# Tower of token features, attention and experts: matmuls regrouped into 64x64 and 32x64 array tiles, accumulator banks exchanged between row halves, periodic features computed ahead of the loop

## Chip, cores, metric

One core of one Trainium2 chip runs the whole program. The metric is the device time of the execution in microseconds (us). The time before is the median of three runs.

## What is computed

Sixteen sequences of 512 tokens, 64 channels. All arithmetic is float32.

```python
# periodic features: 4 id streams, 3 harmonics, sin and cos -> 24 numbers a token
ang = 2*pi*t/period * harmonic + phase;  x = [w*sin(ang), w*cos(ang)]
h   = layernorm(relu(x@W1+b1)@W2+b2)*gamma + beta + 0.1*(x@Wres+bres)
# attention, 8 heads; the context is laid out (head*64+d, position), not the usual way
n = layernorm(h);  k = n@Wk.T;  v = n@Wv.T
attn = softmax(q @ k * scale);  ctx = attn @ v;  h = h + ctx_as_(512,512) through Wo
# top-2 of 6 experts, three 64x64 layers each, gated by a router (64 -> 32 -> 6)
f = layernorm(h);  logits = softmax(relu(f@rw1+rb1)@rw2+rb2);  top 2, softmax of the two
h = h + sum_over_top2(weight * expert(f))
```

## The kernel before

The sequences are handled in eight pairs. `body(i)` in each engine's program walks through 64 slots of pair i. An even slot issues `scores` (L437): four matmuls in 64x64 tiles, each moving 512 columns, into one of three ring buffers `s_bank` (two PSUM banks each). VectorE takes the row maximum of each half (L812) and ScalarE the exponential with its sum (L698), which frees the buffer. Eight slots make one step `a`: 8 x 128 rows of probabilities `p`. For each step `pv` (L464) multiplies the transposed reciprocal sums times output weights (`woz`, made by GpSimd, L300) with `p` into `m_bank`, in two parts of 32 matmuls, at slots 12 and 15 modulo 8. These work in tiles of 128 rows and 32 columns, each matmul moving 128 columns. VectorE then turns `m_bank` into `m` (L824). This is attention re-associated: output weights first, values last. The value product `FIN` (L551) multiplies all of `m` with the values `v` in 16 matmuls of 512 columns into a bank of its own, `f_bank`, and VectorE adds it to `h` as `hatt` (L993).

The other work of the loop is laid into the slots by hand-written tables: `P` for the preparation of pair i+1 (`H1` and `TOK` of the feature network, the layer norms, `T` the transposes at L522, `V` the values), `F` for the rest of pair i-1 (`FIN`, layer norm, `T` transposes L565, `R` router L570, `L` logits L578, `GATE` 22 small VectorE operations, `E1`, `E2`, `Y` expert layers), `Z` the same within the last pair's body, and `L` for the last pair's own tail, after the loop. Before the change `XT` transposes, `R`, `L` and `FIN` use `f_bank`; everything else uses the ring in the order that `ring_order` gives. A matmul that needs a ring buffer waits (`free`) until the entry three places earlier has been read. `m` has one copy only, so the first turn of a pair waits for `FIN` of the pair before (`turn`).

The periodic features (`reduced`, L335, nine VectorE steps, then `sines` on ScalarE and `weigh`) are made in three groups of columns: pair 0 and pair 1 ahead of the loop, 256 columns each, and pairs 2 to 7 (1536 columns) inside `body(0)`, one step every six slots (`FOUR_AT`). A float32 matmul is two instructions in the trace ("passes"), so a count there is twice the count in the code. `warm` issues matmuls on a spare tile whose result nobody reads.

## Time and profile before

| | |
|---|---|
| median of three runs | 755.57 us (755.11 to 757.14) |
| profiled execution | 755.78 us |
| its span | 754.0 us |
| TensorE (PE) busy | 698.5 us, 93% |
| VectorE (DVE) busy | 552.8 us, 73% |
| ScalarE (ACT) busy | 477.7 us, 63% |
| GpSimd (POOL) busy | 289.2 us, 38% |
| start of the first scores | 31.4 us |
| body(0), first scores to first scores of body(1) | 86.6 us |
| body(1) to body(6), each | 86.35 us |
| last body, then the tail | 82.5 us, 35.4 us |

The span is what the profiler saw from the first to the last instruction, 1.8 us less than the execution's own time. Busy shares of TensorE are of modelled ends: two starts in the timeline give a better duration than the length printed for one row.

### The profile page before, as it was taken

The numbers are of one execution on the slowest core, as the hardware profiler recorded it, in microseconds if no ns is written. First come the engines' busy times: TensorE is split into PE (matmuls) and PEld (weight loads), VectorE is DVE, ScalarE is ACT, GpSimd is POOL, SyncE is SP. The second block draws the span as 40 slices with busy tenths as digits, with TensorE's granted clock in tenths as the row PEclk, the third lists the DMA queues.
The fourth block names the chain that finished last, engine by engine and source line by source line (L and its number), as shares of the span: only waits on it lengthen the run. The fifth ranks groups of instructions, "written<-read, shape, count | busy, mean of one in ns | idle before, by whom it ended". The sixth has DMA issues, their size and how long they took to land.

```text
span 754.0 us, 31976 instructions
## 1 busy us (share of the span) xinstructions
PE 698.5 (93%) x14256; PEld 388.7 (52%) x14256; DVE 552.8 (73%) x1069; ACT 477.7 (63%) x1206; POOL 289.2 (38%) x362
## 2 busy tenths in 40 slices
PE   6689879999999999999999999999999999999985
PEld 6344436554555546454554555555455555454662
DVE  6488655878768786877778677777878687677835
ACT  2377675686567766676666766577656875676613
POOL 1143021531566118531466317550376216422702
PEclk9699989999999999999999999999999999999999
DMA  4000000000000000000000000000000000000000
GB/s 167 1 2 3 2 2 3 3 2 3 4 17 3 2 3 3 17 3 2 4 17 3 2 3 4 17 3 3 3 17 3 3 2 4 17 3 3 3 17 16
DMA packets 9449, 7.27 MB, mean 10 GB/s; under 512 B 8672, under 2 KB 8800, under 8 KB 9184
## 3 DMA queue, kind: packets, MB, share of 16 engines
q1 hardware_dynamic: 9312, 5.23, 2.4%
q8 instruction: 112, 1.84, 1.0%
q14 instruction: 25, 0.20, 0.1%
HBM read 3.13 MB, written 2.10 MB: 7 GB/s over the span
## 4 chain that ended last, share of the span: by engine, by line
PE 66%; DVE 17%; ACT 6%; POOL 5%; issue 5%; ACTq 0%; DVEq 0%; POOLq 0%
PE m_bank L464 25%; PE s_bank L437 21%; DVE nmax L812 7%; ACT p L698 4%; PE f_bank L551 3%; PE s_bank L589 3%; PE s_bank L449 3%; PE s_bank L600 2%; PE s_bank L622 2%; DVE st L829 1%; POOL st L1100 1%; DVE e2t L1008 1%; DVE y L1023 1%; PE s_bank L522 1%; PE m_bank L659 1%
## 5 line engine op out<-in xcount | busy, mean ns | idle before, releaser
L698 ACT ACTIVATE p<-s_bank,nmax 128x512 f32<-128x512 f32 x512 | 347.2, 688 | 208.0 <-DVE nmax L812 207.1
L812 DVE TENSOR_REDUCE nmax<-s_bank 128x1 f32<-128x512 f32 x512 | 325.9, 681 | 101.1 <-PE s_bank L437 100.0
L437 PE MATMUL s_bank<-kf,g 64*64 64x512 f32 x2048 | 266.3, 608 | 11.8 <-ACT p L698 8.9
L464 PEld LDWEIGHTS m_bank<-p,woz 128*32 128x32 f32 x8192 | 219.3, 111 | 101.7 <-issue 101.2
L464 PE MATMUL m_bank<-p,woz 128*32 128x128 f32 x8192 | 253.1, 276 | 3.2 <-POOL woz L300 3.1
L300 POOL TENSOR_TENSOR woz<-cst,rz 128x256 f32<-128x256 f32 x126 | 75.9, 624 | 281.2 <-DVE rz L818 281.2
L437 PEld LDWEIGHTS s_bank<-kf,g 64*64 64x64 f32 x2048 | 65.6, 134 | 126.1 <-issue 53.8
L698 ACT ACTIVATION_READ_ACCUMULATOR p<-s_bank,nmax 128x1 f32 x512 | 103.8, 203 | 0.0
L824 DVE STREAM_TRANSPOSE m<-m_bank 128x512 f32<-128x512 f32 x64 | 45.7, 714 | 33.5 <-PE m_bank L464 33.3
L1100 POOL TENSOR_TENSOR st<-st,power 128x8 f32<-128x8 f32 x24 | 40.0, 1668 | 68.8 <-DVE st L839 68.8
L309 POOL TENSOR_TENSOR y<-y,gt 128x768 f32<-128x768 f32 x28 | 41.4, 1477 | 27.9 <-DVE y L1023 26.0
L449 PE MATMUL s_bank<-kf,qk 64*64 64x512 f32 x256 | 35.0, 617 | 8.0 <-ACT p L698 4.9
L1023 DVE TENSOR_TENSOR y<-s_bank,cst 128x768 f32<-128x768 f32 x28 | 26.7, 952 | 15.1 <-PE s_bank L622 11.0
L317 POOL TENSOR_TENSOR ys<-y 128x384 f32<-128x384 f32 x30 | 30.2, 1006 | 17.3 <-DVE y L1034 15.1
L622 PE MATMUL s_bank<-cst,e2t 64*64 64x64 f32 x1536 | 28.7, 220 | 6.6 <-DVE e2t L1008 4.6
L622 PEld LDWEIGHTS s_bank<-cst,e2t 64*64 64x64 f32 x1536 | 25.5, 134 | 17.6 <-issue 13.1
L704 ACT COPY g<-s_bank 128x1024 f32<-128x1024 f32 x32 | 32.4, 1013 | 2.2 <-PE s_bank L449 2.2
L1008 DVE TENSOR_SCALAR e2t<-s_bank,cst 128x512 f32<-128x512 f32 x42 | 29.5, 745 | 4.1 <-PE s_bank L600 4.1
L747 ACT ACTIVATE e1t<-s_bank,cst 128x1024 f32<-128x1024 f32 x24 | 26.7, 1114 | 6.1 <-PE s_bank L589 6.0
L551 PE MATMUL f_bank<-m,v 128*32 128x512 f32 x224 | 27.7, 595 | 0.0
L589 PE MATMUL s_bank<-xt,cst 64*64 64x512 f32 x192 | 26.1, 613 | 1.3 <-ACT p L698 1.3
L709 ACT ACTIVATE sq<-xc 128x512 f32<-128x512 f32 x24 | 15.0, 625 | 18.9 <-DVE xc L851 17.7
(118 smaller groups left out, 499.6 us busy)
## 6 DMA issues: line engine op xcount, KB each, us to landing
tower_out<-o SPq DMA_DIRECT2D x16, 128.0 KB, 2.6
cst<-consts SPq DMA_DIRECT2D x1, 1198.0 KB, 8.9
e2t<-ids SPq DMA_DIRECT2D x1, 896.0 KB, 5.9
cst<-consts SPq DMA_DIRECT2D x1, 544.0 KB, 4.1
cst<-consts SPq DMA_DIRECT2D x1, 288.0 KB, 6.3
e2t<-ids SPq DMA_DIRECT2D x1, 128.0 KB, 2.5
cst<-consts SPq DMA_DIRECT2D x1, 3.5 KB, 2.2
```

What stands on the lines that cost most here:

```text
L300: ops.tensor_tensor(woz[:, kept, four, :].rearrange("q (m h) c -> q m h c", h=2), k("wo").rearrange("q (m c) -> q m c", m=4)[:, 2 * n:2 * ...
L309: ops.tensor_tensor(yt, yt, gt[:, 8, two, :].unsqueeze(3).to_broadcast([128, 2, NE, C]), ALU.mult).then_inc(y_pool, 1)
L437: last = pe.matmul(double[half(q), 512 * r:512 * r + 512], g[half(r), a // 2 % 2, a % 2, first:first + 64], kf[half(r), par, a // 4, :], s ...
L449: last = pe.matmul(double[half(q), 512 * r:512 * r + 512], qk[half(r), 2 * (quad % 2) + q, :], kf[half(r), par, quad // 2, :], start=True, ...
L464: last = pe.matmul(m_bank[quarter(r), 128 * n:128 * n + 128], woz[:, kept, 2 * mm + hh, 32 * oh:32 * oh + 32], keys[:, r, :, :], start=(mm ...
L551: last = pe.matmul(f_bank[quarter(2 * b2 + q), :], v[:, par, b2, jj, quarter(q)], m[:, b2, :, jj, :], start=(jj == 0), stop=(jj == 3))
L589: last = pe.matmul(double[half(q), 512 * r:512 * r + 512], k("e1")[half(r), first:first + 64], xt[half(r), :], start=True, stop=True)
L622: last = pe.matmul(double[half(q), 512 * c + C * x:512 * c + C * x + C], e2t[half(c), x, first:first + 64], k("e3")[half(c), C * x:C * x + ...
L698: nc.scalar.activation(p[:, 8 * kept + c % 8, :], bank("S", i, c - r)[:, 512 * r:512 * r + 512], ACT.Exp, bias=nmax[:, c % 16:c % 16 + 1], ...
L812: nc.vector.tensor_reduce(nmax[:, c % 16:c % 16 + 1], bank("S", i, c - r)[:, 512 * r:512 * r + 512], AX.X, ALU.max, negate=True).then_inc( ...
L824: nc.vector.transpose(m[:, b2, n:n + 4, :, :].rearrange("q n j o -> q (n j o)"), m_bank[:, :]).then_inc(mtd, 1)
L1100: nc.gpsimd.tensor_tensor(st[n][:, 4, :], st[n][:, 3, :], power[:, :], ALU.pow).then_inc(ln_step[n], 1)
```

## The change

In words:
- `pv` works in 64x64 tiles: the 128 rows of `p` are split into two row halves, and each matmul moves 256 columns, 16 matmuls a part. In part 0 row half 0 writes bank `hh=0` of `m_bank` and half 1 bank `hh=1`; in part 1 they swap banks and add, after a wait on `pv_half`. `m_bank` is two banks now, and `f_bank` is gone.
- The second feature layer (`TOK`) does the same exchange (`tok_half`), in 64x64 tiles. The transposes `T` and `XT` become matmuls with an identity in 64x64 tiles (`turn_halves`). The router and the logits are in 64x64 tiles too.
- `FIN` becomes `value_products`: 128 matmuls of 128 columns in 32x64 tiles, in two parts with the exchange wait `fin_half`. It writes two ring buffers, `FIN 0` and `FIN 1`; `XT`, `R` and `L` take a ring buffer each.
- Features: seven steps instead of nine; two groups, pair 0 (256 columns) and pairs 1 to 7 (1792 columns), both ahead of the loop. Four steps of the second group stand before the first layer norm, one in each layer norm, one behind; then VectorE also copies half of `kf` and `g` (`first_copies`). The weighting of the second group is GpSimd's.
- `xn` is stored once instead of twice. The first warm-up has 18 matmuls (24 before), the second 13 (8 before), the second starting one small operation earlier. The slot tables have new numbers.

```diff
-WARM0, WARM, WARM_T = 24, 8, 20
-FOUR_AT, FOUR_SINE, FOUR_WEIGH = (2, 8, 14, 20, 26, 32, 38, 44, 50), 56, 56
+WARM0, WARM, WARM_T = 18, 13, 20
-F = {'FIN': (8, 12, 13, 14),
- 'LN': 14,
+F = {'FIN': 15,
+ 'LN': 15,
...
     def ffn(i, slot, f):
+        if f is not L and slot == f["FIN"]:
+            order.extend([("FIN", i, 0), ("FIN", i, 1)])
+        for name, first in (("XT", "T"), ("R", "R"), ("L", "L")):
+            if slot == f[first]:
+                order.append((name, i))
...
-            if step in (4, 5, 6):
-                ins = stt(out=A, in0=T, scalar=-(c1, c2, c3)[step - 4], in1=A, op0=ALU.mult, op1=ALU.add)
-            if step == 7:
-                ins = ts(A, A, shift, pi, ALU.add, ALU.min)
-            if step == 8:
-                ins = ts(A, A, -pi, None, ALU.max)
+            if step in (4, 5):
+                ins = stt(out=A, in0=T, scalar=-(c1, c2)[step - 4], in1=A, op0=ALU.mult, op1=ALU.add)
+            if step == 6:
+                ins = ts(A, A, least, most, ALU.max, ALU.min)
...
-            def pv(i, a, hh):
+            def pv(i, a, part):
...
-                if hh == 0:
+                if part == 0:
                     wait(pe, mtd, HH * i + a)
                     pe.wait_ge(wozd, 2 * (HH * i + a) + 2)
-                for oh in range(2):
-                    n = 2 * hh + oh
-                    for mm in range(4):
-                        keys = p[:, 8 * kept + 2 * mm + hh, :].rearrange("q (j r o) -> q r j o", j=4, r=4)
-                        for r in range(4):
-                            last = pe.matmul(m_bank[quarter(r), 128 * n:128 * n + 128],
-                                             woz[:, kept, 2 * mm + hh, 32 * oh:32 * oh + 32], keys[:, r, :, :],
-                                             start=(mm == 0), stop=(mm == 3), skip_group_check=True)
-                last.then_inc(pvd, 1)
+                else:
+                    pe.wait_ge(pv_half, HH * i + a + 1)
+                for mm in range(4):
+                    for r in range(2):
+                        hh = (r + part) % 2
+                        keys = p[half(r), 8 * kept + 2 * mm + hh, :].rearrange("q (n h o) -> q h n o", n=8, h=2)
+                        for q in range(2):
+                            last = pe.matmul(m_bank[half(q), 512 * hh:512 * hh + 256], woz[half(r), kept, 2 * mm + hh, :],
+                                             keys[:, q, :, :], start=(part == 0 and mm == 0), stop=(part == 1 and mm == 3),
+                                             skip_group_check=True)
+                last.then_inc(pvd if part else pv_half, 1)
+            def turn_halves(double, part, count):
+                for t in range(count):
+                    for r in range(2):
+                        for c in range(2):
+                            last = pe.matmul(double[half(c), 512 * r + C * t:512 * r + C * t + C], part(t, half(r), c),
+                                             k("ident")[half(r), half(r)], start=True, stop=True,
+                                             skip_group_check=True)
...
+            def value_products(i, par, first, end, part, start, stop):
+                for n in range(8):
+                    for g4 in range(4):
+                        q, s2 = g4 // 2, g4 % 2
+                        odd = (q + part) % 2
+                        for b2 in range(2):
+                            last = pe.matmul(
+                                bank("FIN", i, s2)[half(b2), 512 * odd + 16 * first:512 * odd + 16 * end],
+                                v[quarter(g4), par, b2, n, :],
+                                m[quarter(g4), b2, first + odd:end:2, n, :],
+                                start=(start and n == 0), stop=(stop and n == 7), skip_group_check=True)
...
             def fin_part(n):
...
-                heads, cols = ((slice(0, 8), slice(0, 256)), (slice(8, 12), slice(256, 384)),
-                               (slice(12, 16), slice(384, 512)))[n]
+                first, end = ((0, 4), (4, 6), (6, 8))[n]
...
+                value_products(i, par, first, end, 0, True, False).then_inc(fin_half, 1)
+                pe.wait_ge(fin_half, i + n + 1)
+                value_products(i, par, first, end, 1, False, True).then_inc(fin_parts, 1)
...
-                    for q in range(4):
-                        last = pe.matmul(f_bank[quarter(q), :], k("rw1")[:, quarter(q)], xt[:, :], start=True, stop=True)
+                    free("R", i)
+                    for c in range(2):
+                        for r in range(2):
+                            last = pe.matmul(bank("R", i)[half(c), 512 * r:512 * r + 256], k("rw1")[half(r), half(r)],
+                                             xt[half(r), 256 * c:256 * c + 256], start=True, stop=True)
```

The order of TensorE's matmuls in a body of the loop, slots 7 to 16 of body(1) (`m_bank<-p,woz` is `pv`, `s_bank<-kf,g` scores, `<-kf,qk` a query product, `<-feat,cst` and `<-cst,h1t` the feature network, `<-m,v` the value product; counts are matmuls of the code). Before:

```order
L464 MATMUL m_bank<-p,woz 32x128 x32
L502 MATMUL s_bank<-cst,feat 64x128 x16
L437 MATMUL s_bank<-kf,g 64x512 x4
L511 MATMUL s_bank<-cst,h1t 32x64 x32
L551 MATMUL f_bank<-m,v 32x512 x4
L437 MATMUL s_bank<-kf,g 64x512 x4
L449 MATMUL s_bank<-kf,qk 64x512 x4
L437 MATMUL s_bank<-kf,g 64x512 x4
L464 MATMUL m_bank<-p,woz 32x128 x32
L551 MATMUL f_bank<-m,v 32x512 x8
L437 MATMUL s_bank<-kf,g 64x512 x4
L551 MATMUL f_bank<-m,v 32x512 x4
```

And in the changed kernel, the same slots:

```order
L483 MATMUL m_bank<-p,woz 64x256 x16
L452 MATMUL s_bank<-kf,g 64x512 x4
L531 MATMUL s_bank<-cst,feat 64x128 x16
L546 MATMUL s_bank<-cst,h1t 64x64 x32
L452 MATMUL s_bank<-kf,g 64x512 x4
L464 MATMUL s_bank<-kf,qk 64x512 x4
L452 MATMUL s_bank<-kf,g 64x512 x4
L483 MATMUL m_bank<-p,woz 64x256 x16
L452 MATMUL s_bank<-kf,g 64x512 x4
L483 MATMUL m_bank<-p,woz 64x256 x16
L568 MATMUL s_bank<-m,v 64x128 x128
L452 MATMUL s_bank<-kf,g 64x512 x12
```

The value product moved from three places among the scores (4, 8 and 4 matmuls) into one piece of 128 behind the second part of the products, and its target is the ring.

The order of VectorE's work from the second feature group to the first layer norm, ahead of the loop. Before, with group 1 being pair 1 alone:

```order
L341 TENSOR_SCALAR feat<-e2t,per_turn 128x256
L345 TENSOR_SCALAR feat<-feat,cst 128x256
L347 TENSOR_SCALAR e1t<-feat,cst 128x256
L349 TENSOR_SCALAR e1t<-e1t 128x256
L351 SCALAR_TENSOR_TENSOR feat<-e1t,feat 128x256 x3
L353 TENSOR_SCALAR feat<-feat,cst 128x256
L355 TENSOR_SCALAR feat<-feat 128x256
L361 TENSOR_SCALAR feat<-e1t,cst 128x256
L829 TENSOR_REDUCE st<-s_bank 128x8
L831 TENSOR_SCALAR st<-st 128x8
L851 TENSOR_TENSOR xc<-s_bank,st 128x512
```

And in the changed kernel, the second group, with pieces of the first and second layer norm of pair 0 around it:

```order
L346 TENSOR_SCALAR feat<-e2t,per_turn 128x1792
L350 TENSOR_SCALAR feat<-feat,cst 128x1792
L352 TENSOR_SCALAR e1t<-feat,cst 128x1792
L354 TENSOR_SCALAR e1t<-e1t 128x1792
...
L888 TENSOR_SCALAR st<-st 128x8
L356 SCALAR_TENSOR_TENSOR feat<-e1t,feat 128x1792
L918 TENSOR_TENSOR tok<-xc,cst 128x8x64
L921 TENSOR_TENSOR xc<-tok,st 128x512
...
L356 SCALAR_TENSOR_TENSOR feat<-e1t,feat 128x1792
L901 TENSOR_TENSOR xn<-xc,st 128x512
L358 TENSOR_SCALAR feat<-feat,cst 128x1792
L938 COPY kf<-s_bank 128x512
```

The weighting of pair 1 went to GpSimd, and two 1792-column multiply-adds (L356) stand inside the layer norms, each ahead of an operation that the first transposes wait for.

TensorE's last products and value products, in the tail. Before:

```order
L464 MATMUL m_bank<-p,woz 32x128 x32
L538 MATMUL f_bank<-m,v 32x256 x16
L464 MATMUL m_bank<-p,woz 32x128 x64
L538 MATMUL f_bank<-m,v 32x128 x32
L659 MATMUL m_bank<-spare 128x128 x20
```

And in the changed kernel:

```order
L483 MATMUL m_bank<-p,woz 64x256 x16
L568 MATMUL s_bank<-m,v 64x64 x128
L483 MATMUL m_bank<-p,woz 64x256 x32
L568 MATMUL s_bank<-m,v 64x32 x256
L708 MATMUL m_bank<-spare 128x128 x20
```

The three pieces of the last value product stay where they were, with 128 matmuls each in place of 16.

## Rows read from the trace of the kernel before

**Rows 1.** Windows, bodies 0 and 3: PE, PEld, DVE, ACT, POOL busy, clock, DMA, GB/s.

```profile
31.40:118.00 86.60, 73.97 (x1308) 39.51 (x1312) 61.06 (x97) 59.58 (x147) 20.57 (x23) 0.91 0.01 2
...
290.70:377.05 86.35, 83.69 (x1772) 45.50 (x1764) 66.30 (x130) 58.10 (x149) 38.15 (x48) 1.00 0.02 6
```

**Rows 2.** Timeline of TensorE in body(3): start, length, line, tiles, passes.

```profile
304.23 1.04 PE L449 MATMUL s_bank<-kf,qk 64*64 64x512 f32 x8
305.09 1.04 PE L437 MATMUL s_bank<-kf,g 64*64 64x512 f32 x8
306.06 1.96 PE L464 MATMUL m_bank<-p,woz 128*32 128x128 f32 x64
307.83 1.90 PE L551 MATMUL f_bank<-m,v 128*32 128x512 f32 x16
309.66 1.09 PE L437 MATMUL s_bank<-kf,g 64*64 64x512 f32 x8
310.68 1.06 PE L551 MATMUL f_bank<-m,v 128*32 128x512 f32 x8
311.56 1.93 PE L464 MATMUL m_bank<-p,woz 128*32 128x128 f32 x64
313.42 2.81 PE L437 MATMUL s_bank<-kf,g 64*64 64x512 f32 x24
```

**Rows 3.** The same timeline: logits, expert outputs, both with the next, first feature layer.

```profile
334.38 0.44 PE L578 MATMUL f_bank<-cst,rh 128*32 128x12 f32 x32
334.75 1.09 PE L437 MATMUL s_bank<-kf,g 64*64 64x512 f32 x8
...
375.60 1.63 PE L622 MATMUL s_bank<-cst,e2t 64*64 64x64 f32 x96
377.05 1.90 PE L437 MATMUL s_bank<-kf,g 64*64 64x512 f32 x16
...
382.10 1.09 PE L491 MATMUL s_bank<-feat,cst 64*64 64x256 f32 x16
```

**Rows 4.** TensorE's waits within body(0): in total, times, longest.

```profile
PE s_bank L437 <- ACT p L698: 8.9, 5, 4.8
```

**Rows 5.** Timeline of TensorE in body(0); in brackets idle time ahead and releaser.

```profile
78.38 3.50 PE L464 MATMUL m_bank<-p,woz 128*32 128x128 f32 x64
...
109.93 1.98 PE L437 MATMUL s_bank<-kf,g 64*64 64x512 f32 x8 [4.76 <-ACT p L698]
111.84 3.64 PE L464 MATMUL m_bank<-p,woz 128*32 128x128 f32 x64
```

**Rows 6.** Windows of 7.2 us in body(4), columns as in rows 1.

```profile
398.64:405.83 7.19, 6.87 (x140) 3.65 (x132) 6.87 (x15) 4.53 (x12) 5.65 (x6) 1.00 0.01 2
405.83:413.03 7.20, 6.63 (x108) 3.15 (x108) 6.80 (x12) 4.71 (x14) 2.67 (x4) 1.00 0.00 0
```

**Rows 7.** Ahead of and in body(0): feature steps on VectorE, a copy on ScalarE.

```profile
8.00 0.35 DVE L341 TENSOR_SCALAR feat<-e2t,per_turn 128x256 f32<-128x256 int32 x1
...
12.10 0.41 DVE L361 TENSOR_SCALAR feat<-e1t,cst 128x256 f32<-128x256 f32 x1 [0.48 <-ACT e1t L786]
...
30.36 1.01 ACT L704 COPY g<-s_bank 128x1024 f32<-128x1024 f32 x1 [2.18 <-PE s_bank L449]
...
35.76 1.01 DVE L341 TENSOR_SCALAR feat<-e2t,per_turn 128x1536 f32<-128x1536 int32 x1
...
64.28 1.75 DVE L351 SCALAR_TENSOR_TENSOR feat<-e1t,feat 128x1536 f32<-128x1536 f32 x1
```

**Rows 8.** Timeline of the tail: last products, value products, VectorE's sum.

```profile
716.69 1.91 PE L538 MATMUL f_bank<-m,v 128*32 128x256 f32 x32
...
718.68 3.75 PE L464 MATMUL m_bank<-p,woz 128*32 128x128 f32 x128
...
722.17 2.15 PE L538 MATMUL f_bank<-m,v 128*32 128x128 f32 x64
...
724.39 0.69 DVE L993 TENSOR_TENSOR h<-h,f_bank 128x512 f32<-128x512 f32 x1 [1.20 <-PE f_bank L538]
```

More of the change, by code:

```diff
@@ L540, in fin_part @@
[L540 to L554 removed]
+                    free("FIN", i, 0)
```

365 lines of the change are left out of this document (192 added, 173 removed).

## The prediction

> **What bounds the kernel now.** I read the windows first, one a body of the loop [rows 1]: in body(3) TensorE is busy for 83.69 of 86.35 us at full clock, so it idles 2.66 us, while VectorE is busy for 66.30 and ScalarE for 58.10. body(0) is another case: 73.97 of 86.60 us busy at a mean clock of 0.91, though it has no expert work in it. So the six equal bodies are bound by TensorE, and body(0) partly by something else.
>
> Next the timeline of TensorE, to see what its time is made of. I take start to next start. A product of 512 columns with 64x64 tiles on both sides takes 305.09 - 304.23 = 0.86 us; 0.97 if the next work is in 128x32 tiles; 1.02 with such work on both sides (309.66 to 310.68). A part of the probability product takes 1.77 if the next work has the same tiles (306.06 to 307.83) and 1.86 if it is scores again (311.56 to 313.42) [rows 2]. So leaving one tile shape costs about 0.11 us and entering the next 0.05: 0.16 us a switch, and nearly every part of the products has one on each side. There are 40 switches in each of bodies 1 to 6, 33 in body(0) and 37 in the last (counted in the order of matmuls).
>
> **The change, part by part.**
>
> *Products in 64x64.* Columns moved over tiles are the same: 32 x 128 / 4 before, 16 x 256 / 4 after. Is a 256-column matmul in 64x64 tiles at full rate? The first feature layer is one: its 16 passes, after a switch, have the length of 1.09 us [rows 3] that the 8 passes of 512 columns at 309.66 have after one [rows 2]. So a part costs 1.71 us (two times 0.855), and the products themselves give nothing but their switches. The wait between the two parts costs nothing, since scores stand between them, except in the tail.
>
> *Switches.* In a body, `TOK`, `T`, `XT`, `R`, `L` are in 64x64 too; only the value product (32x64) is left, two switches. 38 x 0.16 = 6.1 us less a body.
>
> *Router.* Four matmuls of 256 columns in place of four of 512, in four tiles: -0.43 us.
>
> *Transposes, logits.* Expert outputs run 96 passes of 64 columns in 377.05 - 375.60 = 1.45 us, 15.1 ns a pass [rows 3]. `T` is 64 such passes, 0.97 us, `XT` 32, 0.48; before they took 1.02 and 0.59 with a switch in each. Nothing to gain or lose, nor for the logits (as many passes as before).
>
> *Value product.* 256 passes of 128 columns in eight tiles. Before: 16 passes in 309.66 - 307.83 = 1.83 us with one switch, so 3.4 for all. No row shows eight tiles or 32 rows. 
>
> Sum for TensorE's work in a body: 83.69 - 6.1 - 0.4 + 0.3 = 77.5 us.
>
> *What is late next.* VectorE keeps its 66.3 us [rows 1], 86% of 77.5, and in the stretch behind the old value product it is already busy for 13.67 of 14.39 us, with TensorE idling 0.89 [rows 6]. Now the value product holds two of three ring buffers for 3.6 us at slot 15; VectorE waits for it with the next turn (one copy of `m`), and turn, sum and mean (each about as long as the sum of 0.69 us in [rows 8]) pile up behind it, ahead of the maxima that free the scores' buffers. So idle time grows. By the rows: the stretch of rows 6 holds 13.50 us of TensorE's work, seven switches (1.1) go from it, and 12.4 stand against VectorE's 13.67, so 1.3 us of waiting; behind the value product one score block (0.86) covers most of turn and first half sum (1.1 to 1.4), 0.4 is left; the waits elsewhere stay at 2.66 - 0.89 = 1.8. That is 3.5 us a body. Low end: the 2.66 of now. High end: if half of the body's work ran like rows 6, 1.3 us of waiting to 12.4 of work, that half had 4.1; with the 0.4, and the 1.8 of elsewhere, it is 6.3. Then a body takes 81.0 us, 5.35 less; six of them **-32.1**.
>
> *The last body* has 35 switches less (5.6), the router's 0.4, and the same new waits (+1): **-5.0**.
>
> *body(0).* Waits of scores for exponentials are 8.9 us in five [rows 4]. 4.8 is the sine in the loop with its two table loads (109.93), the rest but 0.3 stands behind multiply-adds of 1.75 us on VectorE [rows 7]. All go with the features. After the two longest TensorE's clock is down: product parts of 3.50 and 3.64 us in place of 1.96, scores of 1.98 in place of 1.09 [rows 5]; that is 4.1 us. Switches: 33 x 0.16 = 5.3. So 86.6 - 8.6 - 4.1 - 5.3 = 68.6 us. TensorE would then have about 3 us of idle time and 3 of half clock left in it, and VectorE 61.06 - 11.3 = 50 us of work (three steps of 1.75, six of about 1.0 [rows 7]). With 1.2 us of new waits: **-16.8**. If the dense phase costs as much as elsewhere, -14; if the first scores are at full clock, -19.
>
> *Ahead of the loop.* Group 1 took VectorE from 8.00 to 12.51, right up to the first layer norm; four wide steps at 1.01 x 1792 / 1536 = 1.18 us are 4.7 us in the same place [rows 7]: +0.2. Each of the two multiply-adds of 1792 columns costs 1.75 x 1792 / 1536 = 2.0 us, partly under GpSimd's power function: I take +0.5 together, and +0.3 for `T` at half clock. Then one `xn` operation instead of two, -0.8 (one sum's length, 0.7, and a semaphore); `kf` and `g` copied by two engines in place of one, half of 1.01 us [rows 7] each, -1.0. The sine of group 2 stands under the query product. Sum **-0.8**. The weights' product on GpSimd is due five slots later, and hidden.
>
> *The tail.* The three pieces of the value product are 128 matmuls each now, of 64 and 32 columns. At such widths passes cost 11.6 to 15.1 ns whatever they move, 3.0 to 3.9 us a piece. The first took 1.91 [rows 8]; its excess of 1.5 lies partly beside exponentials and `woz`, for which the products behind it wait; I take 1.0. The other two ran from 722.17 to 724.3; now 6.5, +4.3. The exchange in the last products +0.2, router, transposes and six switches -1.0: **+4.5**.
>
> **Sum.** -32.1 - 5.0 - 16.8 - 0.8 + 4.5 = -50.2. The profiled execution's own time was 755.78 us, 0.2 above the median shown; 755.6 - 50.2 = **705.4 us**.
>
> **Rivals.**
>
> *A: VectorE and the ring become the bound.* For it: rows 6, the value product's two ring buffers, and five more ring entries a body. Against: over a whole body VectorE has 11 us to spare even at 77.5, and its waits aren't all bunched. With 7 us of idle time a body instead of 3.5 (from 6.3 on I call it A), seven bodies give back 24: 730 us. The Trainium skill says the same of tiling ("TensorEngine Tiling (Array Packing)", PSUM Bottleneck: it "speeds up TensorE but not PSUM evacuation"). Here the windows say the margin is thin but there.
>
> *B: only four of the eight tiles run side by side.* +3.4 us in each of seven value products = 24, and 3 in the tail: 732 us. For it: no row shows 32-row tiles. Against: everything else obeys columns over tiles.
>
> *C (other side): the row groups of 32 don't overlap at all.* Then two tiles work at once, 53 ns a pass, 13.7 us a value product, +10.2 x 7 = 71, and 3 in the tail: 780 us, slower. It decides from 10.5 us a value product on, 41 ns a pass. Against: 64-row halves do overlap, or the scores would take twice as long.
>
> *D: TensorE's waits stay at 2.66 us a body, and body(0) gains 3 more* (first scores at full clock). 0.84 x 7 + 3 = 9 less: 696 us. For it: the 11 us of slack just named.
>
> **How the numbers follow.** Forecast (700 to 718) 0.56, A 0.16, B 0.10, C 0.03, D 0.12; A and B together 0.03, of which 0.02 within 0.3% and 0.01 slower. The range goes from D's far side to B, 688 to 733, leaving out C, half of what is left of A above it, and the 0.03: about 0.15. Within 0.3% is what a measurement of this kernel can't tell from no change. Faster 0.94, same 0.02, slower 0.04.
>
> **What would show it.** Product parts 1.71 us from start to start, scores 0.86 wherever they stand. The bodies' period 79 to 83 us. A value product of 3.4 to 3.9 us in two pieces; 6.8 is B, 13.7 is C. Idle waits of scores on VectorE or on exponentials, mostly in slots 16 to 28: above 7 us a body is A. body(0) under 72 us without a row of half clock after its first 6 us. From the end of the last products to VectorE's sum 6 to 8 us against 2.2. The prediction is wrong if a product part keeps 1.85 us in spite of one tile shape: then weight loads of 64 columns aren't hidden at 256 columns, and some 20 us come back.

## The result and the profile after

The changed kernel takes 773.58 us (median of 4 runs, 772.83 to 776.52), the kernel before 755.34 beside it: ratio 1.0244, 95% interval 1.0213 to 1.0276. It is slower; the forecast was 705.4 us. The profiled execution took 772.83 us with a span of 771.0, 17.0 more than before. The windows of body(0), body(4) and the last body, against [rows 1] (columns as there):

```profile
32.58:101.61 69.03, 64.42 (x928) 32.48 (x932) 50.69 (x88) 54.16 (x142) 18.38 (x22) 0.98 0.01 2
366.36:455.06 88.70, 80.40 (x1566) 42.61 (x1561) 66.25 (x131) 58.18 (x147) 36.84 (x47) 1.00 0.02 6
632.59:720.96 88.37, 78.64 (x1629) 42.57 (x1621) 61.94 (x123) 52.82 (x139) 37.00 (x52) 1.00 0.04 9
```

body(0) shrank by 17.6 us. A full body has 3.3 us less of TensorE's work than before (80.40 against 83.69), and is 2.3 us longer, since it idles 8.3 us where it idled 2.7. The first piece of the last value product stands ahead of the last products, so its +1.0 of the prediction is counted in the fourth row. Cut into the prediction's terms (from stretch to stretch of both traces):

| stretch | before | after | moved | predicted |
|---|---|---|---|---|
| ahead of the first scores | 31.42 | 32.58 | +1.2 | -0.8 |
| body(0) | 86.6 | 69.0 | -17.6 | -16.8 |
| bodies 1 to 6 | 518.1 | 531.0 | +12.9 | -32.1 |
| last body, up to the last products | 82.6 | 88.4 | +5.8 | -4.0 |
| from there to the end | 35.3 | 50.0 | +14.7 | +3.5 |

TensorE in body(4), around the value product (timeline; in brackets the idle time ahead and its releaser):

```profile
384.89 3.06 PE L568 MATMUL s_bank<-m,v 32*64 32x128 f32 x167
388.79 1.58 PE L568 MATMUL s_bank<-m,v 32*64 32x128 f32 x89 [0.84 <-issue]
390.31 1.09 PE L452 MATMUL s_bank<-kf,g 64*64 64x512 f32 x8
391.62 1.95 PE L452 MATMUL s_bank<-kf,g 64*64 64x512 f32 x16 [0.23 <-DVE hatt L1055]
...
396.01 1.09 PE L452 MATMUL s_bank<-kf,g 64*64 64x512 f32 x8 [0.71 <-ACT p L747]
...
402.47 1.09 PE L452 MATMUL s_bank<-kf,g 64*64 64x512 f32 x8 [1.99 <-ACT p L747]
403.38 1.04 PE L464 MATMUL s_bank<-kf,qk 64*64 64x512 f32 x8
404.74 1.09 PE L452 MATMUL s_bank<-kf,g 64*64 64x512 f32 x8 [0.33 <-ACT p L747]
```

The value product takes 390.31 - 384.89 = 5.4 us, 0.84 of it a gap for which the trace names no releaser ("issue"). Behind it come four waits, 3.3 us; eight more in the rest of the body, of 0.20 to 0.77, make 3.95. The gap has a place of its own: in bodies 1 to 5 it stands behind 252, 224, 195, 167 and 138 of the 256 passes, 28 or 29 earlier from one body to the next. VectorE over the same place:

```profile
390.49 0.72 DVE L873 STREAM_TRANSPOSE m<-m_bank 128x512 f32<-128x512 f32 x1 [5.23 <-PE s_bank L568]
...
391.21 0.70 DVE L1055 TENSOR_TENSOR hatt<-h,s_bank 128x256 f32<-128x256 f32 x2
391.94 0.69 DVE L878 TENSOR_REDUCE st<-hatt 128x8 f32<-128x512 f32 x1
...
392.74 2.48 DVE L861 TENSOR_REDUCE nmax<-s_bank 128x1 f32<-128x512 f32 x4
...
397.84 1.57 DVE L960 SCALAR_TENSOR_TENSOR h<-tok,xc 128x512 f32<-128x512 f32 x1
```

It idles 5.23 us during the value product and has then turn, sums and mean to do before the next maxima. The tail, TensorE's timeline, for [rows 8]:

```profile
715.52 2.48 PE L568 MATMUL s_bank<-m,v 32*64 32x64 f32 x177
719.92 1.11 PE L568 MATMUL s_bank<-m,v 32*64 32x64 f32 x79 [1.93 <-issue]
720.96 4.00 PE L483 MATMUL m_bank<-p,woz 64*64 64x256 f32 x64
724.89 1.35 PE L568 MATMUL s_bank<-m,v 32*64 32x32 f32 x112
727.62 1.95 PE L568 MATMUL s_bank<-m,v 32*64 32x32 f32 x128 [1.38 <-issue]
731.10 0.47 PE L568 MATMUL s_bank<-m,v 32*64 32x32 f32 x16 [1.52 <-issue]
731.78 1.81 PE L568 MATMUL s_bank<-m,v 32*64 32x32 f32 x111 [0.21 <-PE s_bank L568]
735.71 2.42 PE L568 MATMUL s_bank<-m,v 32*64 32x32 f32 x128 [2.12 <-issue]
739.18 0.47 PE L568 MATMUL s_bank<-m,v 32*64 32x32 f32 x17 [1.06 <-issue]
741.29 7.01 PE L708 MATMUL m_bank<-spare 128*128 128x128 f32 x40 [1.64 <-DVE st L878]
```

Two pieces that move 32 columns a pass last 14.9 us, from 724.89 until VectorE's sum begins at 739.76, and six of these are gaps. From the start behind one gap to the start behind the next it is 2.7 to 4.6 us. So two questions: what makes the gaps, and what makes the waits in the bodies?

### The profile page after: what moved, and what is told of

The parts are those of the page before. It is cut to its first block, busy times and chain, and to the rows that moved or that the text cites. A ratio compares the mean times of both kernels' runs of the same rounds, so it can differ in the third digit from the quotient of the medians.

```text
span 771.0 us, 29600 instructions
## 1 busy us (share of the span) xinstructions
PE 675.2 (88%) x13070; PEld 371.0 (48%) x13070; DVE 548.0 (71%) x1064; ACT 472.9 (61%) x1186; POOL 281.3 (36%) x354
## 3 DMA queue, kind: packets, MB, share of 16 engines
q1 hardware_dynamic: 9312, 5.23, 2.3%
q8 instruction: 103, 1.69, 0.9%
## 4 chain that ended last, share of the span: by engine, by line
PE 56%; DVE 23%; issue 7%; ACT 6%; POOL 6%; DMA 1%; SPq 0%; ACTq 0%; DVEq 0%; POOLq 0%
PE m_bank L483 20%; PE s_bank L452 18%; DVE nmax L861 9%; PE s_bank L568 6%; ACT p L747 4%; DVE e2t L1070 3%; PE s_bank L649 2%; PE s_bank L638 2%; PE s_bank L464 2%; DVE y L1085 2%; POOL y L316 2%; DVE st L878 2%; POOL st L1158 1%; DVE h L960 1%; ACT e1t L795 1%
## 5 line engine op out<-in xcount | busy, mean ns | idle before, releaser
L483 PE MATMUL m_bank<-p,woz 64*64 64x256 f32 x4096 | 244.5, 376 | 2.4 <-POOL woz L307 2.3
L483 PEld LDWEIGHTS m_bank<-p,woz 64*64 64x64 f32 x4096 | 158.0, 133 | 119.1 <-issue 67.1
L452 PEld LDWEIGHTS s_bank<-kf,g 64*64 64x64 f32 x2048 | 68.9, 133 | 143.8 <-ACT p L747 50.7
L1158 POOL TENSOR_TENSOR st<-st,power 128x8 f32<-128x8 f32 x24 | 42.9, 1788 | 90.1 <-DVE st L888 90.1
L758 ACT ACTIVATE sq<-xc 128x512 f32<-128x512 f32 x24 | 15.1, 629 | 86.0 <-POOL xc L1153 47.8
L568 PE MATMUL s_bank<-m,v 32*64 32x128 f32 (+2 forms) x2560 | 43.6, 268 | 14.6 <-issue 13.7
L568 PEld LDWEIGHTS s_bank<-m,v 32*64 32x64 f32 x2560 | 37.2, 138 | 22.6 <-issue 19.8
L1085 DVE TENSOR_TENSOR y<-s_bank,cst 128x768 f32<-128x768 f32 x28 | 26.6, 950 | 13.6 <-PE s_bank L671 7.9
L708 PE MATMUL m_bank<-spare 128*128 128x128 f32 x102 | 18.4, 363 | 12.3 <-DVE st L878 11.4
```

Of the source, the lines that this page charges most:

```text
L452: last = pe.matmul(double[half(q), 512 * r:512 * r + 512], g[half(r), a // 2 % 2, a % 2, first:first + 64], kf[half(r), par, a // 4, :], s ...
L483: last = pe.matmul(m_bank[half(q), 512 * hh:512 * hh + 256], woz[half(r), kept, 2 * mm + hh, :], keys[:, q, :, :], start=(part == 0 and mm ...
L568: last = pe.matmul(bank("FIN", i, s2)[half(b2), 512 * odd + 16 * first:512 * odd + 16 * end], v[quarter(g4), par, b2, n, :], m[quarter(g4) ...
L1158: nc.gpsimd.tensor_tensor(st[n][:, 4, :], st[n][:, 3, :], power[:, :], ALU.pow).then_inc(ln_step[n], 1)
```

## The experiments

There are eighteen kernels. A time without a ratio is that of a single execution. A "period" is the time from one body's value product to the next; it is 86.34 us before and 88.5 after.

### Half the matmuls in the value product, and a quarter

`e1_fin64`: 64 matmuls of 256 columns, a bank for each group of rows, no exchange, four half-width sums on VectorE.

```diff
-    bank("FIN", i, s2)[half(b2), 512 * odd + 16 * first:512 * odd + 16 * end],
+    bank("FIN", i, s2)[half(b2), 512 * q + 32 * first:512 * q + 32 * end],
     v[quarter(g4), par, b2, n, :],
-    m[quarter(g4), b2, first + odd:end:2, n, :],
+    m[quarter(g4), b2, first:end, n, :],
```

> The changed kernel with the value product as 64 matmuls of 256 columns in place of 128 of 128: each row group of 32 keeps a bank of its own and works all eight heads, the two partial sums are added by VectorE (four half-width sums in place of two), no exchange wait. Same columns, half the instructions. Theory I (small matmuls outrun the supply of TensorE's instructions): a value product falls from 5.4 us to about 3.6, the gap of 0.8 us in it goes, the two last pieces of the tail from 14.8 to some 7 us; 7 x 1.8 + 8 = about 20 us less, 753 us. Theory II (the tiles of 32 rows don't run eight at a time, whatever the instructions): a value product stays at 4.4 to 5.4 us, 6 to 10 us less from the tail alone. VectorE's two more sums cost up to 0.7 us a body in both.

Measured: 759.66 us (7 runs), ratio 1.0076 (1.0047 to 1.0105), still a little slower than the kernel before. TensorE in two bodies:

```profile
222.51 1.09 PE L452 MATMUL s_bank<-kf,g 64*64 64x512 f32 x8 [1.99 <-ACT p L740]
...
382.42 3.71 PE L565 MATMUL s_bank<-m,v 32*64 32x256 f32 x128
386.06 1.09 PE L452 MATMUL s_bank<-kf,g 64*64 64x512 f32 x8
388.12 1.95 PE L452 MATMUL s_bank<-kf,g 64*64 64x512 f32 x16 [0.96 <-DVE hatt L1049]
...
398.95 1.86 PE L452 MATMUL s_bank<-kf,g 64*64 64x512 f32 x8 [1.99 <-ACT p L740]
```

The value product is 3.64 us and its gap is gone, but the sums are now waited for 0.96 us, and the waits behind stay. The period is 87.65 in bodies 1 and 2, and 88.8 in the next three: there the scores behind the same 1.99 us run at half clock (1.86 in place of 1.09, granted clock 0.55). Most of the 15 us gained is the tail's: from its first piece to the end 44.1 us instead of 55.5. Theory I had the value product and the gap right; of its 20 us, the waits for the sums and the half clock took back a part.

`e2_fin_quarter`: the changed kernel with `for n in (0, 7)` in place of `range(8)`. It leaves out three quarters of the value product.

> The changed kernel with a quarter of the value product's matmuls (two of eight groups of keys; the rest is left out, so the attention's sum is incomplete). Theory III (the value product in one piece holds VectorE and ScalarE up, and the waits of scores behind it come from that): a body loses the 4.1 us of the piece and 2 to 3 us of waits behind it; with 13 us in the tail 712 us. Theory IV (the waits come from the ring's new entries XT, R and L and stay): 4.1 x 7 + 13 = 42 less, 731 us.

Measured: 731.16 us, period 85.1, with the waits behind it still 0.30, 1.03, 1.99 and 0.33. With a quarter of the value product left, a body is 3.4 us shorter, and the waits stay. That is Theory IV's number, but not yet its cause: whether the entries of the ring make the waits is asked below.

### The gaps by themselves

Spare matmuls take the place of, or follow, the 20 in front of `XT` in the tail, where nothing else runs.

```diff
+for cols in (32, 128):
+    for n in range(512):
+        r, q = n // 2 % 2, n % 2
+        pe.matmul(m_bank[half(q), 512 * r:512 * r + cols], spare[half(r), 0:64],
+                  spare[half(r), 0:cols], start=True, stop=True, skip_group_check=True)
```

That is the first of them; a matmul is two passes in the trace.

`e8_supply` (64 rows, 32 and then 128 columns):

> The changed kernel with its 20 spare matmuls in the tail replaced by 512 spare ones of 32 columns and then 512 of 128 columns, in 64x64 tiles, all four tiles in rotation, nothing to wait for and no other work on the chip beside them. Theory of supply: TensorE gets its instructions 256 at a time, and passes that are shorter than the supply leave gaps labelled issue after every 128 passes (two instructions each), at both sizes; the tail of the changed kernel had 112 to 128 passes every 2.7 to 4.6 us, so each group of 512 takes 11 to 18 us, the 32 columns not much less than the 128. Rival, that the passes themselves are the limit: 512 at the 17.2 ns of the value product are 8.8 us for 128 columns and less for 32, with no gaps. The whole is some 20 to 35 us longer than the changed kernel.

`e12_supply32` (64 rows, then 32 rows, of two row groups):

> The changed kernel with spare matmuls behind the 20 of the tail: first 256 of 128 columns in tiles of 64 rows, then 256 of 128 columns in tiles of 32 rows (512 passes each; a matmul is two passes). Supply theory: about 3.7 us for each 128 passes whatever the tile, 15 us a group, 30 together, and the passes of 32 rows show larger gaps, since they run at 17 ns when they run. Rival, that loading 64 rows of weights sets the 27 ns a pass seen in the run before: the group of 32 rows takes 512 times 17.2 ns, 8.8 us, with no gaps. The whole: 773 plus 28 to 32, or plus 22 to 24.

`e16_supply_first32` (32 rows first):

> The changed kernel with 256 spare matmuls of 128 columns in tiles of 32 rows behind the 20 of the tail, and then 256 in tiles of 64 rows: the order of the earlier run turned round. Supply theory: 27.8 us for 1024 passes as before in total; the first 100 to 128 passes of 32 rows, whose instructions are already there, run at 17 ns each, and then come gaps or the steady 27 to 28 ns. Rival, that 27 to 28 ns is what such a pass costs TensorE: 27.8 ns from the first pass on, and no gap.

Measured: 825.63, 801.15 and 802.95 us. In `e12_supply32`, 64 rows and then 32:

```profile
748.05 14.25 PE L606 MATMUL m_bank<-spare 64*64 64x128 f32 x512
762.23 14.43 PE L610 MATMUL m_bank<-spare 32*64 32x128 f32 x512
```

`e17_supply_four` uses four groups of rows with a bank each, so eight tiles, as the value product does:

> The changed kernel with 512 spare matmuls (1024 passes) of 128 columns behind the 20 of the tail, in tiles of 32 rows and now over all four groups of rows with a bank each, as the value product has them; the earlier runs used two groups of rows and went at 27 to 28 ns a pass from the first on, with a gap of 0.23 us after each 128 only late. Supply theory: as in the value product, the first 128 or so go at 17 ns, then a gap ends each 128, 3.5 to 3.75 us from one start to the next, 28 to 30 us for the 1024: 801 to 803 in all. Rival, that two groups of rows made the 27 ns and the supply never binds: 17.2 ns throughout, 17.6 us, no gaps, 790 to 792.

```profile
749.44 3.09 PE L606 MATMUL s_bank<-spare 32*64 32x128 f32 x199
753.50 2.08 PE L606 MATMUL s_bank<-spare 32*64 32x128 f32 x128 [0.97 <-issue]
756.97 2.08 PE L606 MATMUL s_bank<-spare 32*64 32x128 f32 x128 [1.39 <-issue]
760.72 2.08 PE L606 MATMUL s_bank<-spare 32*64 32x128 f32 x128 [1.66 <-issue]
```

Measured: 800.9 us. This is the supply: 199 passes, 13.8 ns from one start to the next, and from then on a gap, 128 passes in 2.08 us, a gap, and the next 128, 3.47 or 3.75 us from start to start, six times over. 128 passes are 256 instructions (weights and matmul). The page of the changed kernel's profile counts what was fetched for all engines:

```profile
q8 instruction: 103, 1.69, 0.9%
```

1.69 MB in 103 packets is 16.4 KB each. The trace of `e17_supply_four` has these packets one by one. All the DMA traffic from 753.4 to 776.9 us, in 40 slices and by queue:

```profile
GB/s 0 28 0 0 0 0 0 28 0 0 0 0 0 0 28 0 0 0 0 0 28 0 0 0 0 0 28 0 0 0 0 0 28 0 0 0 0 0 28 0
q8 instruction: 7, 0.11, 2.0%
```

There are seven gaps, the first just ahead of this stretch, and seven packets in it, one in each group of passes. A packet starts 1.05 to 1.15 us after its group has begun, takes 0.9 to 1.4 us, and the next group begins 1.2 to 1.6 us after it has ended: together the 3.5 to 3.75 us. The DMA engines are 2% busy meanwhile, so what is waited for looks like a round trip and not like a full DMA queue. In the value product of body(4) a packet ends at 387.44 and the gap at 388.79. And the gap follows the count of instructions, not the time: in all seven value products it stands behind the same number of passes in `e10_max_half`, `e11_exp_half` and `e19_both_half`, whose bodies are 0.8 to 4 us shorter.

The Trainium skill ("Runtime: NRT & Kernel Launch", Instruction fetch mechanics) says that instructions are fetched in blocks of 16 KiB, 256 instructions, and that this is hidden since engines dispatch more slowly than blocks arrive. The block agrees with the gaps. That it is hidden does not hold here, where TensorE takes 256 instructions in 2.08 us and gets them every 3.47 or 3.75.

### The entries of the rotation

`e4_before_ring`: the kernel before, with `XT`, `R` and `L` in the rotation.

```diff
+        for name, first in (("XT", "T"), ("R", "R"), ("L", "L")):
+            if slot == f[first]:
+                order.append((name, i))
```

> The kernel before with another part alone: the transposes XT, the router R and the logits L take a ring buffer each, the value product keeps its own bank. Theory IV (ring entries): at least 1 us of new waits a body, 762 us or more. Theory III (the value product's piece): under 0.5 us a body, within 755 to 759 us.

Measured: 799.11 us, ratio 1.0575 (1.0543 to 1.0608), period about 92.5. Its largest new wait:

```profile
338.88 1.99 PE L446 MATMUL s_bank<-kf,g 64*64 64x512 f32 x8 [2.57 <-ACT rh L769]
```

In the old order of the work three more entries cost 6 us a body. New waits are 4.3 of them; behind the one shown the clock is granted at 0.50, and the scores take 1.99 us in place of 1.09. Is it so in the changed kernel? `e5_xt` and `e7_all` start from `e1_fin64` and take `XT`, or `XT`, `R` and `L`, out again, into the bank of the products between two fillings.

```diff
-            if slot == f[first]:
+            if slot == f[first] and not (f is F and name in IN_M_BANK):
...
+                    pe.wait_ge(mtd, turned[0])
```

> The version with the value product in 64 matmuls (759.7 us), with the turns of the mixture (XT) of six bodies taken out of the rotation: they go to the bank of the products between two of its fillings (PE waits for the transpose of the products before, the next products wait for the copy of XT). One entry of the rotation less in each of six bodies. Ring-entry theory: the six together cost about 6 us a body in the old kernel, 1.5 to 2 us an entry, so 9 to 12 us less: 748 to 751, with the waits of the scores for exponentials (21.8 us over the run) down to 14 or less. Rival, that the waits come from the value product and the layer norm alone and go wherever there is room: 757 to 762. Rival, that the bank of the products is too tight a place: the products wait for the copy of XT about 1 us a body, 760 to 766.

> The same with all three of XT, R and L of six bodies outside the rotation, in the bank of the products between its fillings; XT two slots later, R one earlier, L two later, and the gates one slot later. Three entries less a body: by the ring-entry theory what the old kernel lost by them (43 us over the run, 6 us in each of seven bodies) comes back in six bodies, less what the products now wait: 725 to 738. Rival (the waits come from elsewhere): 757 to 762. Rival (new waits of the products for R's and L's readers, 1 us each): 745 to 755.

Measured: 762.05 (ratio 1.009, 1.0071 to 1.0109) and 760.94 us (1.007, 1.0052 to 1.0088). The waits of scores for exponentials fell from 21.8 to 9.8 and 9.2 us over the run, and more was waited for the place instead (15.7 us in six bodies). In `e7_all`:

```profile
402.18 1.13 PE L507 MATMUL m_bank<-cst,x 64*64 64x64 f32 x32 [2.61 <-DVE m L880]
```

`e9_none` adds an empty entry behind `R`, for which PE waits and which it doesn't use:

> The version with the value product in 64 matmuls, with one empty entry more in the rotation behind R in each of six bodies: no matmul uses it, PE only waits until it would be free. Ring-entry theory: one more entry costs what one costs elsewhere, 1.5 to 2 us a body, 769 to 772. Rival (entries cost nothing, work and its readers do): 758 to 762.

Measured: 758.81 us, period 88.3. This entry costs at most 0.7 us a body (88.3 against 87.65), and nothing in the whole. I had thought after `e4_before_ring` that the number of entries was the cause; in the changed kernel neither this entry more nor the one and three fewer of `e5_xt` and `e7_all` bear that out. That the 6 us in the old one came from where the readers stood in its order (`R`'s copy three slots behind `R`) is argued from the wait above and wasn't tried alone.

### Whose work is late

`e10_max_half`, `e11_exp_half` and `e19_both_half`: the changed kernel with maxima, exponentials, or both, over 256 of 512 columns.

```diff
...
-    bank("S", i, c - r)[:, 512 * r:512 * r + 512], AX.X, ALU.max, negate=True)
+    bank("S", i, c - r)[:, 512 * r:512 * r + (256 if i else 512)], AX.X, ALU.max, negate=True)
```

> The changed kernel with the maxima of the scores taken over 256 of the 512 columns in all bodies but the first (the other half isn't looked at): the same matmuls, entries and exponentials, VectorE some 20 us a body lighter. The entries of the rotation have been found to cost nothing by themselves, so what is asked is who is late when PE waits 7 to 8 us a body. Theory VectorE (the maxima queue behind its layer norm, gate and sum instructions, and exponentials and PE follow): most of the waits go, 5 us or more in each of seven bodies, 730 to 740. Rival ScalarE (exponentials of 0.89 us are themselves the pace): 765 to 773. Rival, the path through both (each shortening helps in part): 745 to 760.

> The changed kernel with the exponentials taken over 256 of the 512 columns in all bodies but the first (the products then read older values in the other half): the same matmuls, entries and maxima, ScalarE some 16 us a body lighter. Theory VectorE: little changes, 760 to 773. Rival ScalarE: the waits for exponentials go, 730 to 745. Rival, the path through both: 745 to 760.

> The changed kernel with both the maxima and the exponentials taken over 256 of the 512 columns in all bodies but the first (what lies in the other half isn't looked at, and the products read older values there). Alone, the first gave 22 us and the second 6. Theory of the round from scores to maxima to exponentials to the free entry: the waits are paid where that round is longer than PE's own work in two pairs of scores, so both together give more than the sum of 28, and the waits of the scores for exponentials nearly go: 728 to 740. Rival, that each engine was the limit in places of its own: the sum, 743 to 747. Rival, that what was left is neither's (the layer norm's, gates' and experts' own instructions and the order they stand in): 748 to 752, no more than the maxima alone gave.

Measured: 750.91, 767.29 and 743.7 us, spans 21.9, 5.5 and 29.1 shorter: nearly the sum. Periods 85.7, 87.7 and 84.6. One body of the first and of the third in windows:

```profile
347.01:432.61 85.60, 80.10 (x1552) 42.76 (x1553) 48.88 (x131) 57.79 (x147) 36.81 (x46) 1.00 0.03 6
```

```profile
343.83:428.22 84.39, 79.67 (x1552) 43.61 (x1553) 48.89 (x131) 45.05 (x147) 36.81 (x46) 1.00 0.03 6
```

VectorE lost 17 us of work in a body and the body became 2.9 shorter; ScalarE lost 13 and it became 0.8 shorter. With both, 4.7 us of idle time are left, of the 8.3. The same halves in the kernel before were not tried, so these numbers name who is late now, and not how much of it the change brought.

### Other places for the same work

`e14_lnb_later` (from `e1_fin64`) puts the next pair's second layer norm, 3.1 us on VectorE behind the value product, four slots later with all that follows it. `e15_split_merge` adds: the value product in two halves with a pair of scores between, its sums two slots later, and in the tail one piece in place of the last two. `e18_lnb_t_later` is the first with `T` and `V` eight slots later (39 and 41), and the tail's merged piece.

```diff
- 'LNB': 21, 'SQB': 23, 'LNB2': 27, 'T': 31, 'V': 33
+ 'LNB': 25, 'SQB': 27, 'LNB2': 31, 'T': 35, 'V': 37
...
```

> The version with the value product in 64 matmuls (759.7 us), with the second layer norm of the next pair put four slots later (and its squares, scaling, transposes and values with it): about 3.1 us of VectorE work a body leave the 11 us behind the value product, where VectorE is busy 95% of the time, for a stretch in which it is busy half of the time. Dense-stretch theory: the waits of the scores for exponentials of 0.70, 1.99 and 0.33 us a body (3.0 us in six bodies) mostly go, 2 to 3 us a body, 742 to 749. Rival, that the waits come from the number of entries or from the value product's block alone: 757 to 762. Rival, that the four slots later collide with the gates and experts: the waits only move, 755 to 762, with the waits for gt and e1t above 0.7 and 0.4 us.

> The same with three more: the value product in two halves with one pair of scores between (so VectorE and ScalarE have work during it, where VectorE idles 3.5 and ScalarE 6.8 us now), its readers two slots later, the first gate step one slot earlier; and in the tail the last two pieces of the value product made one, half as many matmuls. Theory: block and supply both cost. The block 1 us a body in six bodies, the gate's wait 0.5 a body, the tail 3 us (128 passes at the supply's 3.6 us instead of 256): 9 to 12 us less than with the layer norm alone, 732 to 740. Rival, that the readers being later starve the scores of entries: the wait for hatt grows from 0.96 to over 2 us and the bodies gain nothing, only the tail's 3 us: 740 to 747.

> The version with the layer norm of the next pair four slots later once more, but with its transposes and values eight slots later instead of four, since the run before had PE wait 3.0 us a body for the scaled tokens, which GpSimd makes behind a product of the weights that it does in order; and with the tail's last two pieces of the value product in one, which took 3.0 us from the last products to the sum where the two pieces took 7.0. Dense-stretch theory: the waits for exponentials behind the value product fall from 3.0 to 2.2 us a body (as they did in that run, 0.70, 1.19 and 0.33), the 3.0 for the tokens goes, the tail gives 4: 747 to 753. Rival, that the layer norm must stay where it is, since whoever is later (GpSimd's chain, then the transposes, the values, the experts) gives the wait back: 760 to 775 in spite of the tail's 4 us.

Measured: 785.52 (ratio 1.0401, 1.0381 to 1.0421), 798.66 (1.0593, 1.0544 to 1.0642) and 774.1 us (1.0259, 1.0225 to 1.0293). The wait of 1.99 became 1.19 in the first and the third, and each opened a larger one. In this order, the transposes in `e14_lnb_later` and the queries in `e18_lnb_t_later`:

```profile
430.30 1.16 PE L493 MATMUL s_bank<-cst,xn 64*64 64x64 f32 x64 [3.01 <-POOL xn L1154]
```

```profile
435.78 1.28 PE L464 MATMUL s_bank<-kf,qk 64*64 64x512 f32 x8 [2.10 <-DVE e2t L1062]
```

In `e15_split_merge` the sums that come two slots later are waited for 3.2 us a body. All three forecasts of a gain missed: the wait moved by hand reappeared elsewhere, larger. The rivals had this in kind, but 785.52 and 798.66 us lie above every range that was given. The tail's merged piece alone (in `e15_split_merge`) did what was expected: from the end of the last products to VectorE's sum 3.0 us (762.66 to 765.64) against 7.0 in `e1_fin64` (717.99 to 724.98) and 14.9 in the changed kernel.

### The features alone

`e3_before_features`: the kernel before, with only the features in seven steps ahead of the loop. `e13_before_best` adds the changed kernel's 18 and 13 spare matmuls and the split of the first query copy.

```diff
-            for step in range(9):
+            for step in range(4):
                 reduced(dve, nc.vector, 1, step)
-            weigh(dve, nc.vector, 1)
...
```

> The kernel before with one part of the change alone: the features of pairs 1 to 7 in seven steps ahead of the loop. In the changed kernel body(0) fell from 86.6 to 69.0 us, of which I put 5.3 to tile switches; so body(0) here is 74 us, the time ahead of it 1 to 2 us longer, 755 - 12 + 1.5 = 745 us. If instead the sine and the wide steps cost only what their own busy time is, less than 6 us come off.

> The old kernel with the features ahead of the loop (745.8 us) and, from the changed kernel, 18 and 13 spare matmuls there, the second group one step earlier, and the first query copy split between VectorE and ScalarE. With its 8 spare matmuls the transposes and the first queries ran at half clock, 1.94 and 1.98 us; with 13 the changed kernel ran them at full clock. Theory: 0.9 us each for the two, 0.9 of the scores that follow and 0.3 of the copy, so 3 us less, 741 to 744. Rival: the spare matmuls end before the transposes either way and the clock stays low: 745 to 746. Faster than the old kernel in both cases.

Measured: 745.82 us, ratio 0.9873 (0.9857 to 0.989), and 745.23 us, 0.9866 (0.9847 to 0.9885), which can't be told apart. Periods 86.3 as before; the first scores start at 35.62 and 35.43, 4 us later than before, and what follows until the first value product takes 14.1 us less. The 745 us of the first forecast were met with both terms larger than it had them (1.5 and 12.6), which is partly luck. The transposes of `e3_before_features` and of `e13_before_best`:

```profile
29.33 1.94 PE L519 MATMUL s_bank<-cst,xn 128*128 128x128 f32 x8 [3.42 <-DVE xn L882]
```

```profile
29.45 1.94 PE L523 MATMUL s_bank<-cst,xn 128*128 128x128 f32 x8 [2.49 <-DVE xn L887]
```

Both run at half clock. In `e3_before_features` the granted clock was 0.50 all the way from the spare matmuls. In `e13_before_best` it had risen to 1.00 in them, was still so at 29 us, and was 0.58 on average from 29 to 30 us, where the transposes start after 2.49 us of idle time. In the changed kernel, with 1.61 us idle at that place, it stayed at 1.00. So the rival was right there: the 18 and 13 spare matmuls gained nothing. These are the two fastest kernels that compute everything, and both beat the old one and the changed one.

## Why the prediction was wrong

**Right.** *Products*: a part takes 1.72 us from start to start (the sum had 1.71), scores 0.86; the switches are gone. *body(0)*: 69.0 us against 69.8, and `e3_before_features` shows most of it to be the features'. *Value product, eight tiles side by side*: they do work side by side; rivals B (6.8 us) and C (13.7) are out. At 256 columns a pass takes 27.0 ns from start to start where 26.7 are ideal (`e1_fin64`), at 128 it takes 13.6 to 14.5 where 13.3 are. The step was only somewhat too small: 3.7 us stood in the sum, and 4.6 came out without the gap. The exchange wait puts 0.33 us between two passes, and each part starts slowly (16.8 ns a pass for the first 16). The Trainium skill's figure for four groups of rows, 3.07 times one ("TensorE: Matmul & The Clock Gate", Part 3), gave an estimated 4.4 us and so came nearer than my 3.7, but by luck: the passes themselves run at 3.9 times one (4 x 13.3 / 13.8).

**Wrong: "What is late next", 3.5 us of waits a body.** It is 8.3, in seven bodies. The step added up two places and left the rest as it was: "the waits elsewhere stay at 1.8". They became 3.95, eight small ones; behind the value product 3.3 stood instead of 1.7; the gap in the value product is the last 0.8. Also each wait costs 0.23 us beyond its length (0.18 of drain, since a product of 1.04 us overlaps the next by that, and 0.05 of start: 403.38 - 402.47 is 0.91 and not 0.86), and six more waits and the gap are 1.6 us. So a body is 7.5 us over its term: 4.8 of idle time, 1.6 of restarts, 0.7 of value product (without its gap's restart), 0.4 unexplained. Six bodies are 45 us of the 67 missed, the last body 9.8 (2.4 of it the first piece of its value product). That was rival A, VectorE and the ring. I had priced it at 7 us of idle time, without restarts, and given it 0.16. The runs name its parts: half of VectorE's maxima is worth 2.9 us a body, half of ScalarE's exponentials 0.8, and the two nearly add up; one more entry of the ring cost no more than 0.7, where it was tried. So VectorE is the larger part, and the number of entries, as far as it was tried, is not the cause. Of the 8.3, 4.7 are left with both halved, 0.2 to 1.3 of it the supply's gap. The rest are waits for expert layers and their sums, for exponentials, and for gates. In `e18_lnb_t_later` other places made two of them worse (for the gates 0.69 to 1.32, for the second expert layer 0.46 to 2.10); that no order of this work could avoid them was not shown.

**Wrong: the tail, +4.5 us, and "+1.0" for its first piece.** What follows the last products is 14.7 us longer, not 3.5, and the first piece grew from 2.0 to 5.4, by 3.4 and not 1.0. The term took passes as TensorE runs them, 11.6 to 15.1 ns. Where no gap is, they ran at 7 to 17 ns, but the supply gives 27 to 29 ns a pass over a long row of them. `e17_supply_four` shows that rate without any value product, and the merged piece shows what it is worth, 4 us for 128 passes saved.

**Wrong by 2.0 us: ahead of the loop.** First scores start at 32.58, not 30.6. The step that failed is "+0.5 together" for the two multiply-adds of 1792 columns, "partly under GpSimd's power function". After, and then before:

```profile
16.13 2.02 DVE L356 SCALAR_TENSOR_TENSOR feat<-e1t,feat 128x1792 f32<-128x1792 f32 x1
16.37 3.29 POOL L1158 TENSOR_TENSOR st<-st,power 128x8 f32<-128x8 f32 x1 [15.41 <-DVE st L888]
24.49 3.35 POOL L1158 TENSOR_TENSOR st<-st,power 128x8 f32<-128x8 f32 x1 [4.83 <-DVE st L888]
...
16.00 1.96 POOL L1100 TENSOR_TENSOR st<-st,power 128x8 f32<-128x8 f32 x1 [15.03 <-DVE st L839]
22.78 1.64 POOL L1100 TENSOR_TENSOR st<-st,power 128x8 f32<-128x8 f32 x1 [4.82 <-DVE st L839]
```

Beside the multiply-add the power function takes 1.33 and 1.71 us longer, and the layer norm waits for it: 3.0 us in place of 0.5. `e3_before_features`, which has only the features changed, starts these two layer norm steps within 0.1 us of the same times. The first layer norm also starts 0.4 us later (0.2 in the sum), and from the scaling in the second one to the scores it is 2.3 us less (1.5 in the sum).

**Gains that were there and were lost.** TensorE's work fell by 3.3 us a body as measured, and some 5 without the restarts. None of it made a body shorter, because the chain from scores through maxima and exponentials back to the free buffer now sets the pace in places. The Trainium skill's sentence quoted in rival A ("TensorEngine Tiling (Array Packing)", PSUM Bottleneck), that tiling speeds up TensorE and not the emptying of PSUM, describes it, and the trace agrees: VectorE, which reads the scores out of PSUM, kept its 66.25 us in body(4) (66.30 before), while TensorE's work shrank.

## What to carry to other kernels

Here TensorE had 3% of slack, and saving some 6% of its work made its readers the bound. Price the waits of the whole body, not of one place, and add 0.2 us for each restart. Count instructions as well as columns: here runs of passes of 8 to 17 ns met a first gap after 112 to 252 of them, and a long row of them went at 27 to 29 ns a pass, so half as many of twice the width cost nothing. Split a mixed change first: one of its parts alone made the kernel 1.3% faster, where the whole made it 2.4% slower.

## What the runs showed of the hardware

- Supply: TensorE ran through 199 passes of 32x64 tiles, 13.8 ns apart, and was then fed 128 at a time (256 instructions, one packet of 16.4 KB), every 3.47 or 3.75 us (`e17_supply_four`).
- Columns over tiles: at 2.4 GHz a pass of 128 columns takes 27.3 ns with four tiles in use, whether they have 64 or 32 rows (`e12_supply32`), and 13.8 with eight (`e17_supply_four`); one of 256 columns takes 27.0 with eight (`e1_fin64`). At 1.2 GHz one of 128 columns with four tiles takes 54 ns (`e8_supply`).
- Two engines: an 8-column power function on GpSimd took 3.3 us beside a 1792-column multiply-add on VectorE, and 1.6 to 2.0 without. Why was not tried.
